# Opening handed on by tiles and halves, and POOL's follow-up steps placed a slot later, in a four-block transformer kernel

## Chip, core and metric

One core of a Trainium2 chip. The time is the device time of one execution in microseconds (us). Engines: PE (TensorE, matrix products), DVE (VectorE), ACT (ScalarE), POOL (GpSimd) and SP, which issues the transfers.

## What is computed

x has 4 batches of 512 tokens with 128 channels. Four residual layers follow each other; each first normalises x over its channels.

```python
x = x + attn_a(layernorm(x))   # channel attention, 8 heads of 16 channels: rms norm, q and k normalised over tokens
x = x + ffn(layernorm(x))      # 8 experts of 336 hidden, a router, a small actor net that says how many experts count
x = x + attn_b(layernorm(x))   # token attention, one head, scores times a step function of sigmoid
x = x + ffn(layernorm(x))      # the same expert weights again

# attn_a
q, k = l2norm(q), l2norm(k)    # over the tokens
sim  = einsum('bhin,bhjn->bhij', q * exp(temperature), k)
out  = einsum('bhij,bhjn->bhin', softmax(sim), v) @ w_out.T
# ffn
scores = where(rank < sampled_k, softmax(x @ router_w.T), 0)
for e in range(8):
    out += scores[..., e] * ((silu(x @ gate_w[e].T) * (x @ up_w[e].T)) @ down_w[e].T)
```

## The kernel before

The main loop is the expert layer. Its 8 x 336 hidden units are 21 chunks of 128, and it runs over 8 blocks: block n is batch n of the first expert layer for n below 4, batch n - 4 of the second one behind. So there are 168 slots, k = 21 n + c. In a slot PE makes the gate product and the up product of chunk c (`gu k`), each as three float32r products of high and low halves (`three`, L1007 to L1009, 128 x 512 elements), and a down product of an earlier chunk in float32 (`down k`, L1157, two records for one product). ACT makes silu of the gate product into `sl` (L691), DVE multiplies the up product into `t2` (`uk k`, L953), POOL makes the second multiplication of `t2` in place (`um k`, L574), and the down product reads that. In blocks 0 to 2 (`ROUTED_LATE`) DVE multiplies by silu and POOL by the routing weights `sbc`; from block 3 on DVE multiplies by `sbc` and POOL by silu. The gate product of slot k needs silu k - 2, since two banks of PSUM alternate, and the up product needs `uk k - 2`.

Everything else is cut into steps that a planner, `plan` (L163), puts between the slots. The lists `A_STEPS`, `B_STEPS`, `F_STEPS` give for each step a slot from the start of its thread; `COST` and `POOL_COST` are rough costs by which a step is put off or a product `um` is let in. Each engine then walks the one common list of steps and issues its own share of each step, so the place of a step in the list is its place in every engine's queue. An engine that waits for a semaphore in one step holds up all that it has behind. The steps that matter here:

- `stats` (DVE mean and variance, L786 and L789), with POOL's reciprocal root in the same step (L519 to L524: from the fourth normalisation on four instructions, a multiplication, an affine, a power and a product). `xn` normalises: on DVE for the first three (L800), on ACT for the others (L594). `xT` transposes it on PE (L1027), ACT copies it as the high half (L614), `xl` makes the low half on DVE (L819).
- `ag`, `ar`, `asim` (PE L1040, L1048, L1055 and L1057): Gram product of xn, its product with the weights of q and k, the similarity with the sums of squares of q and k beside it. `ass` (DVE L842) takes the sums, POOL's power (L533) stands in the same step. `ascale` (DVE L849 qn and L850 simT) scales, `asT` transposes simT on PE (L1063), `amax`, `aexp`, `awo` (L872 the output weights), `am` (PE L1069), `am2`, `y` (PE L1085) and the addition to x (DVE L878) follow.
- `route` (PE L1097 and L1098): the router's products. They need the low halves of x and of the router's weights (`swl`, DVE L809 and L810). `actk` (DVE L937) ends in the choice of experts; POOL spreads it to the weights `sx` (L543) in the same step, and `sbc` transposes them.
- `warm`: products of the identity on PE (L1019), 12, 2, 4, 7 and 10 of them, whose results are not read.

`PRELUDE` (L75) is the opening, written out by hand: attention of batch 0, statistics of batch 1, and the normalisation of block 0 up to its low half. PE's other small products take turns in three banks of PSUM (4 to 6); `turn(t)` waits until the one three turns back is free. At its start POOL sets up the identity and constants; the head mask `hmask` of 24 small instructions (L491 to L494) comes after the first reciprocal root.

## Time and profile before

| | |
|---|---|
| median of 3 runs | 499.86 us (499.83 to 501.45) |
| the profiled execution | 500.62 us, span of its profile 498.8 us |
| PE busy | 484.0 us, 97% of the span |
| DVE, ACT, POOL busy | 294.1, 243.4, 292.1 us |

A row of the timeline has the start in us from the span's start, the length in us, the engine, the line, the operation, the tile written and the tiles read, the shape, and how many instructions are merged in it; in brackets the engine's idle time just before and what ended it. A float32 product of PE makes two records. PEld is PE's weight load. In a table of windows the stretch comes first, then its length, the busy time and count of each engine, and behind them PE's granted clock (1.00 is 2.4 GHz, 0.50 is 1.2 GHz).

### The profile page before, as it was taken

The page shows a single profiled execution, that of the slowest core. Times are in us where ns is not written, and L with a number is a line of the kernel's source. Part 1 is how long each engine was busy: PE and PEld are TensorE (multiplying, and loading weights), DVE is VectorE, ACT ScalarE, POOL GpSimd, SP SyncE. Part 2 cuts the span into 40 slices and gives each one's busy share as a digit, 9 for nine tenths or more (in the row PEclk, how much of TensorE's full clock was granted, in tenths as well). Part 3 has the DMA queues.
Part 4 walks back from the last instruction along what each step waited for, and adds up shares of the span by engine and source line. Part 5 has one row for each costly group of instructions (what it writes and reads, how often), then busy time and mean ns, then how long its engine had stood idle before and what let it go on. Part 6 is the DMA issues. An engine that isn't in the chain of part 4 may idle for free.

```text
span 498.8 us, 6344 instructions
## 1 busy us (share of the span) xinstructions
PE 484.0 (97%) x2035; PEld 340.1 (68%) x2035; DVE 294.1 (59%) x695; ACT 243.4 (49%) x437; POOL 292.1 (59%) x307
## 2 busy tenths in 40 slices
PE   7798899999999899999999999999999999999997
PEld 7676767677666666676676676667676676666666
DVE  3538343746768795497937985469763334623232
ACT  3185837457624874248742756326671344232221
POOL 4346779338868485464563656365563646655653
PEclk9899999999999999999999999999999999999999
DMA  8700000000000000000000000000000000000000
GB/s 240 237 0 2 0 1 1 0 1 1 1 1 1 1 0 1 0 1 1 0 1 1 0 2 0 1 0 24 0 1 0 1 23 0 0 1 21 1 1 21
DMA packets 7932, 7.36 MB, mean 15 GB/s; under 512 B 732, under 2 KB 7772, under 8 KB 7900
## 3 DMA queue, kind: packets, MB, share of 16 engines
q1 hardware_dynamic: 7900, 6.97, 4.6%
q8 instruction: 16, 0.26, 0.2%
q14 instruction: 16, 0.13, 0.1%
HBM read 5.91 MB, written 1.05 MB: 14 GB/s over the span
## 4 chain that ended last, share of the span: by engine, by line
PE 81%; DVE 2%; ACT 1%; issue 1%; POOL 0%; ACTq 0%; DVEq 0%
PE bank L1157 26%; PE bank L1007 15%; PE bank L1009 14%; PE bank L1008 14%; PE bank L1195 3%; PE bank L1187 1%; PE bank L1111 1%; PE bank L1027 1%; PE bank L1165 1%; PE bank L1207 1%; PE bank L1119 1%; PE bank L1145 1%; PE bank L1098 1%; PE bank L1097 0%; PE bank L1085 0%
## 5 line engine op out<-in xcount | busy, mean ns | idle before, releaser
L574 POOL TENSOR_TENSOR t<-t,sl 128x512 f32<-128x512 f32 x105 | 136.0, 1299 | 109.8 <-DVE t L953 93.4
L691 ACT ACTIVATE sl<-bank 128x512 f32<-128x512 f32 x168 | 99.3, 597 | 150.0 <-PE bank L1009 143.5
L1157 PE MATMUL bank<-t,WD 128*128 128x512 f32 x328 | 162.7, 591 | 0.0
L953 DVE TENSOR_TENSOR t<-bank,sbc 128x512 f32<-128x512 f32 x105 | 72.4, 690 | 93.7 <-PE bank L1009 92.5
L1007 PE MATMUL bank<-xhF,WGh 128*128 128x512 f32 x168 | 103.8, 618 | 3.0 <-ACT sl L691 2.2
L574 POOL TENSOR_TENSOR t<-t,sbc 128x512 f32<-128x512 f32 x63 | 81.9, 1326 | 11.2 <-ACT sbc L685 7.9
L1157 PEld LDWEIGHTS bank<-t,WD 128*128 128x128 f32 x328 | 61.8, 188 | 25.1 <-issue 13.0
L953 DVE TENSOR_TENSOR t<-bank,sl 128x512 f32<-128x512 f32 x63 | 42.8, 685 | 54.7 <-ACT sl L691 24.3
L1007 PE MATMUL bank<-xhF,WUh 128*128 128x512 f32 x168 | 66.5, 396 | 1.3 <-DVE t L953 1.3
L1009 PE MATMUL bank<-xhF,WGl 128*128 128x512 f32 x168 | 66.3, 395 | 0.0
L1009 PE MATMUL bank<-xhF,WUl 128*128 128x512 f32 x168 | 66.0, 393 | 0.0
L1008 PE MATMUL bank<-xlF,WGh 128*128 128x512 f32 x168 | 65.9, 392 | 0.0
L1008 PE MATMUL bank<-xlF,WUh 128*128 128x512 f32 x168 | 65.6, 390 | 0.0
L1007 PEld LDWEIGHTS bank<-xhF,WGh 128*128 128x128 f32 x168 | 31.8, 189 | 26.2 <-issue 21.1
L1008 PEld LDWEIGHTS bank<-xlF,WGh 128*128 128x128 f32 x168 | 31.8, 190 | 21.5 <-issue 19.9
L1007 PEld LDWEIGHTS bank<-xhF,WUh 128*128 128x128 f32 x168 | 31.5, 188 | 10.4 <-DVE t L953 3.5
L1009 PEld LDWEIGHTS bank<-xhF,WGl 128*128 128x128 f32 x168 | 31.5, 187 | 7.5
L1008 PEld LDWEIGHTS bank<-xlF,WUh 128*128 128x128 f32 x168 | 31.6, 188 | 7.2
L1009 PEld LDWEIGHTS bank<-xhF,WUl 128*128 128x128 f32 x168 | 31.5, 188 | 7.2
L691 ACT ACT_TABLE_LOAD x19 | 24.4, 1283 | 0.3
L519 POOL TENSOR_SCALAR nm<-mv 128x4 f32<-128x4 f32 x13 | 3.0, 230 | 26.6 <-DVE mv L789 26.5
L521 POOL TENSOR_TENSOR rstd<-rt,nhalf 128x4 f32<-128x4 f32 x16 | 16.6, 1035 | 1.3
(191 smaller groups left out, 636.8 us busy)
## 6 DMA issues: line engine op xcount, KB each, us to landing
stage<-in_gate SPq DMA_DIRECT2D x7, 192.0 KB, 6.1
stage<-in_up SPq DMA_DIRECT2D x7, 192.0 KB, 6.3
WD<-in_down SPq DMA_DIRECT2D x7, 192.0 KB, 6.2
X<-in_x SPq DMA_DIRECT2D x4, 256.0 KB, 5.5
out<-X SPq DMA_DIRECT2D x3, 256.0 KB, 2.3
raw<-in_small SPq DMA_DIRECT2D x1, 388.0 KB, 4.6
out<-X SPq DMA_DIRECT2D x2, 128.0 KB, 1.9
raw<-in_small SPq DMA_DIRECT2D x1, 192.0 KB, 2.7
```

The costliest lines, as they stand in the source:

```text
L521: r = pool.tensor_tensor(rstd[:, :], rt[:, :], nhalf[:, :], ALU.pow)
L574: pool.tensor_tensor(t2[k % NT2][:, :], t2[k % NT2][:, :], by[:, :], ALU.mult).then_inc(a_done, 1)
L691: act.activation(sl[k % NSL][:, :], bank[k % 2][:, :], ACT.Silu).then_inc(silu_done, 1)
L953: dve.tensor_tensor(t2[k % NT2][:, :], bank[2 + k % 2][:, :], by[:, :], ALU.mult).then_inc(t2_done, 1)
L1007: pe.matmul(out, lh, rh, start=start, stop=False)
L1008: pe.matmul(out, lh, rl, start=False, stop=False)
L1009: return pe.matmul(out, ll, rh, start=False, stop=stop)
L1027: r = pe.transpose(m[:, i * P:i * P + P], xn[:, i, :], ident[:, :])
L1098: r = pe.matmul(m[:, o + 2 * E:o + 3 * E], xl[:, a], router[:, 0:E], start=True, stop=True)
L1111: r = pe.matmul(m[:, 8 * i:8 * i + KMAX], hq[:, i * P:i * P + P], w2[:, 0:KMAX], start=True, stop=True)
L1157: pe.matmul(OACC[:, :], WD[:, c, :], t2[k % NT2][:, :], start=(c == 0), stop=(c == CH - 1 or k == TAIL[0] - 1))\
L1195: r = pe.matmul(m[:, :], xnB[b % 2][:, j, :], PT[:, j, :], start=(j == 0), stop=(j == NT - 1))
```

## The change

POOL's share of three steps becomes a step of its own: `rstd` (the reciprocal root), `apow` (the power of the norms) and `sx` (the spread of the experts' weights). In the lists they stand a slot behind the step that they were part of, before the step that reads them; `ascale` of batches 2 and 3 moves a slot too. In the opening the results are passed on in parts: xn of the first three normalisations by tiles; the sums of squares of batch 0 ahead of the similarity and in a bank of their own; y of batch 0 in four banks, added and measured by tiles; the transposed x of block 0 in two halves, with the first gate product's order changed so that both parts which need only the high half come first. Half of the head mask is made before the first reciprocal root.

```diff
-A_STEPS = [(0, "stats"), (2, "xn"), ... (8, "ass"), (9, "ascale"),
+A_STEPS = [(0, "stats"), (1, "rstd"), (2, "xn"), ... (8, "ass"), (9, "apow"), (10, "ascale"),
...
-POOL_COST = dict(wp=1.2, wc=1.5, um=1.4, stats=1.4, ass=.8, bqkl=1.4, actk=1.1, inner=1)
+POOL_COST = dict(wp=1.2, wc=1.5, um=1.4, rstd=1.4, apow=.8, bqkl=1.4, sx=1.1, inner=1)
...
             pool.memset(nhalf[:, :], -0.5).then_inc(consts_ready, 1)
+            head_mask(range(H // 2))
...
-                if kind == "stats":
+                if kind == "rstd":
...
                     if seq == 0:
-                        head_mask()
-                if kind == "ass":
+                        head_mask(range(H // 2, H)).then_inc(consts_ready, 1)
+                if kind == "apow":
...
-                if kind == "actk":
+                if kind == "sx":
...
+                    if (what, b) == ("F", 0):
+                        act.wait_ge(half_full, 1)
+                        act.activation(xhF[0][:, 0:T // 2], bank[3][:, 0:T // 2], ACT.Copy).then_inc(xh_half, 1)
...
                     for i in range(NT):
-                        r = dve.tensor_scalar(xn[:, i, :], X[:, NT * q + i, :], mv[:, i, 0:1], rstd[:, i:i + 1],
-                                              ALU.subtract, ALU.mult)
-                    r.then_inc(xn_ready, 1)
+                        dve.tensor_scalar(xn[:, i, :], X[:, NT * q + i, :], mv[:, i, 0:1], rstd[:, i:i + 1],
+                                          ALU.subtract, ALU.mult).then_inc(xn_ready, 1)
...
+                    if s == ("y", 0):
+                        for i in range(NT):
...
+                            r = dve.tensor_tensor(X[:, i, :], bank[i][:, 0:P], X[:, i, :], ALU.add)
...
+                    to = m if b else bank[1]
                     for j in range(2):
-                        r = pe.matmul(m[:, P + j:P + j + 1], qsq[:, 1 - j, :], ones[:, :], start=True, stop=True)
+                        r = pe.matmul(to[:, P + j:P + j + 1], qsq[:, 1 - j, :], ones[:, :], start=True, stop=True)
+                    if b == 0:
+                        r.then_inc(squares_full, 1)
+                        r = pe.matmul(m[:, 0:P], raw[:, C_QKV + P:C_QKV + 2 * P], gw[:, 0, :], start=True, stop=True)
...
+                    if k == 0:
+                        pe.wait_ge(xh_ready, split_no["F", 0] + 1)
+                        pe.matmul(bank[0][:, :], WGh[:, 0, :], xhF[0][:, :], start=True, stop=False)
+                        pe.matmul(bank[0][:, :], WGl[:, 0, :], xhF[0][:, :], start=False, stop=False)
```

What this does to the engines' queues behind the opening shows in three places. DVE, slots 16 to 18, the scaling of batch 2 (qn, simT) among the multiplications `uk` into the sixteen buffers t2 (t20 is that of slot 16, t21 of slot 17); before:

```order
89 L842 TENSOR_SCALAR ss_139<-bank5 128x2
90 L953 TENSOR_TENSOR t20_114<-bank2,sl0_112 128x512
91 L786 BN_STATS bst_83<-X_49 128x6 x4
92 L789 BN_AGGR mv0_84<-bst_83 128x2 x4
93 L849 TENSOR_TENSOR qn_144<-rs_140,etemp_69 128x1
94 L850 TENSOR_SCALAR simT_141<-bank5,rs_140 128x128
95 L953 TENSOR_TENSOR t21_115<-bank3,sl1_113 128x512
96 L953 TENSOR_TENSOR t22_116<-bank2,sl0_112 128x512
```

and now:

```order
93 L867 TENSOR_SCALAR ss_139<-bank5 128x2
94 L990 TENSOR_TENSOR t20_114<-bank2,sl0_112 128x512
95 L802 BN_STATS bst_83<-X_49 128x6 x4
96 L805 BN_AGGR mv0_84<-bst_83 128x2 x4
97 L990 TENSOR_TENSOR t21_115<-bank3,sl1_113 128x512
98 L875 TENSOR_TENSOR qn_144<-rs_140,etemp_69 128x1
99 L876 TENSOR_SCALAR simT_141<-bank5,rs_140 128x128
100 L990 TENSOR_TENSOR t22_116<-bank2,sl0_112 128x512
```

The scaling now stands behind the multiplication of slot 17. The same happens to batch 3 in slots 34 to 36. PE's queue still has the transposition of simT (`asT`) at its old place, behind the transposes of block 1.

PE, slots 48 to 49, the transposes of block 3 (ident, xn), which stood right behind the products of slot 49; before:

```order
436 L1009 MATMUL bank<-xhF_75,WGl 128x512
437 L1007 MATMUL bank<-xhF_75,WUh 128x512
438 L1008 MATMUL bank<-xlF_77,WUh 128x512
439 L1009 MATMUL bank<-xhF_75,WUl 128x512
440 L1027 MATMUL bank<-ident,xn_79 128x128 x4
441 L1007 MATMUL bank<-xhS,zh 128x512
```

and now:

```order
436 L1046 MATMUL bank<-xhF_75,WGl 128x512
437 L1044 MATMUL bank<-xhF_75,WUh 128x512
438 L1045 MATMUL bank<-xlF_77,WUh 128x512
439 L1046 MATMUL bank<-xhF_75,WUl 128x512
440 L1217 MATMUL bank<-t_121,WD 128x512
441 L1067 MATMUL bank<-ident,xn_79 128x128 x4
442 L1044 MATMUL bank<-xhS,zh 128x512
```

Down product 39 has gone ahead of the transposes; it had stood a slot later. In the same way down product 23 is now ahead of the transposes of batch 0 for the second attention (slot 36) and of `asT` behind them.

POOL, slots 62 to 64, the reciprocal root of block 4 (nm, rt, rstd, nmr) among the products `um` (t215 is that of slot 63, t20 of slot 64); before:

```order
166 L574 TENSOR_TENSOR t214_128<-t214_128,sbc0_110 128x512
167 L519 TENSOR_SCALAR nm0_90<-mv0_84 128x4
168 L520 TENSOR_SCALAR rt0_88<-mv0_84 128x4
169 L521 TENSOR_TENSOR rstd0_86<-rt0_88,nhalf_72 128x4
170 L524 TENSOR_TENSOR nmr0_92<-nm0_90,rstd0_86 128x4
171 L574 TENSOR_TENSOR t215_129<-t215_129,sl1_113 128x512
172 L574 TENSOR_TENSOR t20_114<-t20_114,sl0_112 128x512
```

and now:

```order
166 L578 TENSOR_TENSOR t214_128<-t214_128,sbc0_110 128x512
167 L578 TENSOR_TENSOR t215_129<-t215_129,sl1_113 128x512
168 L578 TENSOR_TENSOR t20_114<-t20_114,sl0_112 128x512
169 L523 TENSOR_SCALAR nm0_90<-mv0_84 128x4
170 L524 TENSOR_SCALAR rt0_88<-mv0_84 128x4
171 L525 TENSOR_TENSOR rstd0_86<-rt0_88,nhalf_72 128x4
172 L528 TENSOR_TENSOR nmr0_92<-nm0_90,rstd0_86 128x4
```

Two products now stand ahead of the root, and each of them waits for DVE's multiplication of its slot. ACT's queue has the same steps in the same places in both kernels; only the copy of block 0's high half is now two.

## Rows read from the trace of the kernel before

**Rows 1.** The page, busy time by engine, share of the span, instructions.

```profile
PE 484.0 (97%) x2035; PEld 340.1 (68%) x2035; DVE 294.1 (59%) x695; ACT 243.4 (49%) x437; POOL 292.1 (59%) x307
```

**Rows 2.** PE's waits from 27 us: total us, times, longest us.

```profile
PE bank L1007 <- ACT sl L691: 2.2, 2, 1.7
```

**Rows 3.** Windows of the opening; PE's granted clock is behind POOL.

```profile
15.00:16.00 1.00, 1.00 (x6) 1.00 (x6) 0.50 (x3) 0.43 (x2) 0.00 (x0) 0.50 1.09 354
```

**Rows 4.** Timeline, attention of batch 0 in the opening.

```profile
6.37 1.11 DVE L800 TENSOR_SCALAR xn<-X,mv,rstd 128x128 f32<-128x128 f32 x4 [1.52 <-POOL rstd L521]
...
7.54 1.16 PE L1040 MATMUL bank<-xn 128*128 128x128 f32 x8 [0.52 <-DVE xn L800]
...
10.92 0.46 PE L1055 MATMUL bank<-gw,raw 128*128 128x128 f32 x2 [0.65 <-DVE qsq L833]
...
11.22 0.50 PE L1057 MATMUL bank<-ones,qsq 128*128 128x1 f32 x4
...
11.76 0.16 DVE L842 TENSOR_SCALAR ss<-bank 128x2 f32<-128x2 f32 x1 [0.98 <-PE bank L1057]
...
12.11 0.34 POOL L494 TENSOR_SCALAR_AFFINE_SELECT hmask<-hmask 128x16 f32<-128x16 f32 x1
12.41 0.70 POOL L533 TENSOR_TENSOR rs<-ss,nhalf 128x2 f32<-128x2 f32 x1
...
13.89 3.19 PE L1019 MATMUL bank<-ident 128*128 128x128 f32 x14
...
15.66 0.28 DVE L872 TENSOR_SCALAR wo<-raw,ari 128x128 f32<-128x128 f32 x1
...
16.88 0.43 PE L1069 MATMUL bank<-wo,attn 128*128 128x128 f32 x2
```

**Rows 5.** Timeline, from y of batch 0 to the first routing product.

```profile
18.55 1.16 PE L1085 MATMUL bank<-mixw,xaT 128*128 128x128 f32 x8 [0.37 <-ACT mixw L653]
...
19.74 0.69 DVE L878 TENSOR_TENSOR X<-bank,X 128x512 f32<-128x512 f32 x1 [2.16 <-PE bank L1085]
...
24.41 1.10 PE L1027 MATMUL bank<-ident,xn 128*128 128x128 f32 x8 [0.44 <-DVE xn L800]
...
25.11 0.60 ACT L614 ACTIVATE xhF<-bank 128x512 fp32r<-128x512 f32 x1 [0.35 <-PE bank L1027]
...
26.99 0.28 DVE L810 TENSOR_TENSOR SWl<-raw,SWh 128x128 fp32r<-128x128 f32 x1
...
28.04 0.17 PE L1097 MATMUL bank<-router,xhF 128*128 128x16 f32 x1
```

**Rows 6.** Timeline, slots 17 to 19: normalisation of block 1, transposition of batch 2's similarity.

```profile
70.10 1.65 ACT L594 ACTIVATE xn<-X,nmr,rstd 128x128 f32<-128x128 f32 x4 [4.05 <-POOL nmr L524]
...
72.30 0.27 PE L1063 MATMUL bank<-ident,simT 128*128 128x128 f32 x1
...
72.32 1.29 DVE L953 TENSOR_TENSOR t<-bank,sl 128x512 f32<-128x512 f32 x2 [3.99 <-issue]
```

**Rows 7.** Timeline, slots 34 to 37: scaling of batch 3, next gate product.

```profile
119.57 1.27 POOL L574 TENSOR_TENSOR t<-t,sbc 128x512 f32<-128x512 f32 x1
...
119.63 1.22 DVE L849 TENSOR_TENSOR qn<-rs,etemp 128x1 f32<-128x1 f32 x1 [0.50 <-POOL rs L533]
...
123.49 0.50 PE L1007 MATMUL bank<-xhF,WGh 128*128 128x512 f32 x1 [0.51 <-ACT sl L691]
```

**Rows 8.** Timeline, slots 49 to 51: high half, down products, routing product of block 3.

```profile
161.20 0.60 ACT L614 ACTIVATE xhF<-bank 128x512 fp32r<-128x512 f32 x1 [0.54 <-PE bank L1027]
...
163.08 1.88 PE L1157 MATMUL bank<-t,WD 128*128 128x512 f32 x4
...
167.97 0.28 PE L1097 MATMUL bank<-router,xhF 128*128 128x16 f32 x1 [0.76 <-DVE xlF L819]
```

**Rows 9.** Timeline, slots 65 to 68: normalisation of block 4, silu behind it, a gate product.

```profile
217.64 1.64 ACT L594 ACTIVATE xn<-X,nmr,rstd 128x128 f32<-128x128 f32 x4
...
219.18 0.58 ACT L691 ACTIVATE sl<-bank 128x512 f32<-128x512 f32 x1
...
222.97 0.48 PE L1007 MATMUL bank<-xhF,WGh 128*128 128x512 f32 x1
```

More of the change, by code:

```diff
@@ L398, in build @@
         xn_act = sem("xn_act")
+        half_full, xh_half = sem("half_full"), sem("xh_half")
+        squares_full = sem("squares_full")
+        y0_tile, x0_tile = sem("y0_tile"), sem("x0_tile")
         m_full = [sem(f"m_full{i}") for i in range(3)]
@@ L427, in wait_free, with wait_xn @@
             eng.wait_ge(m_free[t % 3], t // 3 + 1)
-        def wait_xn(eng, seq):
+        def wait_xn(eng, seq, tile=NT - 1):
             if seq < DVE_NORMS:
-                eng.wait_ge(xn_ready, seq + 1)
+                eng.wait_ge(xn_ready, NT * seq + tile + 1)
             else:
@@ L485, in chain, with head_mask @@
                 pool.wait_ge(pool_did, did[0])
-            def head_mask():
-                for e in range(H):
+            def head_mask(heads):
+                for e in heads:
                     own = hmask[:, e * DH:e * DH + DH]
@@ L613, in _ @@
                     dst = xhF[b % 2] if what == "F" else xhS
+                    if (what, b) == ("F", 0):
+                        a = slice(T // 2, T)
+                        act.activation(dst[:, a], m_bank(t)[:, a], ACT.Copy).then_inc(xh_ready, 1)
+                        continue
                     act.activation(dst[:, :], m_bank(t)[:, :], ACT.Copy).then_inc(xh_ready, 1)
@@ L777, in _ @@
                         dve.wait_ge(x_loaded[q], 16)
-                    else:
+                    elif (what, b) != ("F", 0):
                         wait_free(dve, turn_of[src])
@@ L785, in _ @@
                     for i in range(NT):
+                        if (what, b) == ("F", 0):
+                            if i < NT - 1:
+                                dve.wait_ge(x0_tile, i + 1)
+                            else:
+                                wait_free(dve, turn_of[src])
                         r = dve.bn_stats(bst[:, i, :], X[:, NT * q + i, :])
@@ L815, in _ @@
                     dst, hi = (xlF[b % 2], xhF[b % 2]) if what == "F" else (xlS, xhS)
+                    if (what, b) == ("F", 0):
+                        a = slice(0, T // 2)
+                        dve.wait_ge(xh_half, 1)
+                        dve.tensor_tensor(dst[:, a], bank[3][:, a], hi[:, a].bitcast(F32), ALU.subtract)
+                        a = slice(T // 2, T)
+                        dve.wait_ge(xh_ready, split_no["F", 0] + 1)
+                        dve.tensor_tensor(dst[:, a], m_bank(t)[:, a], hi[:, a].bitcast(F32), ALU.subtract).then_inc(n_free(t), 1)
+                        continue
                     dve.wait_ge(xh_ready, split_no[what, b] + 1)
@@ L1022, in _ @@
                     t = turn_of[s]
-                    wait_xn(pe, norm_no[what, b])
-                    xn = xnB[b % 2] if what == "B" else xns[norm_no[what, b] % 2]
+                    seq = norm_no[what, b]
+                    xn = xnB[b % 2] if what == "B" else xns[seq % 2]
                     m = turn(t)
                     for i in range(NT):
-                        r = pe.transpose(m[:, i * P:i * P + P], xn[:, i, :], ident[:, :])
+                        if i == 0 or seq < DVE_NORMS:
+                            wait_xn(pe, seq, i if seq < DVE_NORMS else NT - 1)
+                        to = bank[3] if (what, b) == ("F", 0) and i < NT // 2 else m
+                        r = pe.transpose(to[:, i * P:i * P + P], xn[:, i, :], ident[:, :])
+                        if (what, b, i) == ("F", 0, NT // 2 - 1):
+                            r.then_inc(half_full, 1)
                     r.then_inc(m_full[t % 3], 1)
@@ L1084, in _ @@
                         a = slice(i * P, i * P + P)
-                        r = pe.matmul(m[:, a], xaT[b % 2][:, a], mixw[:, :], start=True, stop=True)
+                        to = m[:, a] if b else bank[i][:, 0:P]
+                        r = pe.matmul(to, xaT[b % 2][:, a], mixw[:, :], start=True, stop=True)
+                        if b == 0 and i < NT - 1:
+                            r.then_inc(y0_tile, 1)
                     r.then_inc(m_full[t % 3], 1)
@@ L1130, in _ @@
                         pe.wait_ge(silu_done, k - 1)
-                    three(bank[k % 2][:, :], WGh[:, c, :], WGl[:, c, :], xh, xl).then_inc(g_full, 1)
+                    if k == 0:
+                        r = pe.matmul(bank[0][:, :], WGh[:, 0, :], xl, start=False, stop=True)
+                    else:
+                        r = three(bank[k % 2][:, :], WGh[:, c, :], WGl[:, c, :], xh, xl)
+                    r.then_inc(g_full, 1)
                     if k >= 2:
```

56 lines of the change are left out of this document (35 added, 21 removed).

## Prediction, made before the changed kernel was run

> **What bounds the kernel now.** I read the page's busy shares first: TensorE (PE) is busy 484.0 of 498.8 us, no other engine over 60% [rows 1]. So past the opening only what makes PE wait can change the time. The waits of PE after 27 us come next; the largest is for ScalarE's silu, twice, 2.2 us in all [rows 2]. Third, the timeline of the opening: there PE works through a chain of small steps in which one engine hands to the next, and fills the gaps with warm-up products of the identity that nobody reads. Steps that end earlier there move the whole main loop. Fourth, the timeline at the places where the planner's order is different. The granted clock of PE in the opening is the last view: from 15 to 16 us it is 0.50, the 1.2 GHz level [rows 3].
>
> **The opening, part by part.** (a) *xn passed on by tiles.* DVE writes four tiles of xn in 1.11 us from 6.37, and the Gram product starts only at 7.54, eight records in 1.16 us [rows 4]. With 0.27 for the last record that is 0.11 per record. Now it ends two records after the fourth tile, not eight: 6 x 0.11 = 0.67 us earlier. The warm-up ahead of it is nearly done when the first tile comes, so the last tile decides. (b) *Squares first.* The two column sums start 0.30 after the 128-wide product in front of them (10.92 and 11.22). They now stand ahead of it: 0.30. (c) *Half of the head mask before the statistics.* The norms' sums end at 11.92, but POOL's power starts at 12.41, behind the last select of the mask (12.11 for 0.34) [rows 4]. The handover from DVE to PE at 7.48 and 7.54 costs under 0.1, so 0.4 comes free. Half of the mask moves into POOL's wait for the first statistics, so the other half is done well ahead of the power. (d) *The warm-up in front of the attention's product.* The weights of the output product are ready at 15.94 (15.66 plus 0.28), the product starts at 16.88: fourteen warm-up records took 3.19 us, 0.21 each, at half clock [rows 3, 4]. With the chain 1.4 earlier they start at 12.5 and end between 14.1 (all at the higher level) and 14.5 (the fall again near 13.5), before the weights at 14.6. Another 0.86 goes. (e) *y in tiles.* One addition of 0.69 follows the eight records of y [rows 5]. In four parts, the last one overhangs by a quarter plus its fixed cost, some 0.2 to 0.3: 0.5 with the handover. (f) *Halves of the transposed x.* ScalarE copies it from 25.11 for 0.60, DVE makes the low part, then PE starts the first gate product. In halves that path is up to 1.3 shorter. But the routing product at 28.04 also needs the low router weights, which DVE finishes at 27.27 behind the squares of batch 1 [rows 5]; those wait for ScalarE's other copies, which start only 0.3 earlier. So PE gains 28.04 - 27.27 - 0.1 + 0.3 = 0.95, and I take that.
>
> Sum: 0.67 + 0.30 + 0.40 + 0.86 + 0.50 + 0.95 = 3.7 us. The upper bound is 4.0 (1.3 for the last term). Below: the second long warm-up, ten products in twenty records, stands in front of batch 1's Gram product and the transposes. If the low clock falls on it, each record costs 0.1 more, 2 us; over half of that has cover, since PE still waited for xn behind it, 0.44 us before the transposes at 24.41 [rows 5] and more before the Gram product. I count 0.8. Before the fall of 13.5 PE had worked in short pieces; the new chain has its thin stretch, the same three small products, just ahead of that warm-up. I take 3.4 us, between 3.7 and 2.9.
>
> **The steps moved to a later slot.** Most of it costs nothing: for the expansion of the weights POOL had been idle, so products now go first. Three places are not free.
>
> *First place, the second scaling (batch 2), slots 16 to 18.* DVE now has product 17's multiplication ahead of qn and simT. That multiplication waits for silu 17, and silu 17 stands on ScalarE behind a normalisation (70.10 for 1.65). It ran at 72.32 [rows 6]. PE takes simT at 72.30, right after the transposes. Before, simT was ready long ahead. Now it comes at 72.32 + 0.61 (the next issue) + 0.4 = 73.35, so PE waits 1.1 us, and nothing behind it has slack, as PE is never idle there. Ends: 1.1, and 2.2 if qn is held up.
>
> *Second place, the third scaling, slots 34 to 36.* The same: the multiplication ahead of it waits for a silu, and PE itself waited 0.51 for that silu at 123.49 [rows 7]. simT comes near 124.6, PE goes on at 124.75. A down product (0.86) now stands ahead and fills PE's gap, so the loss is 124.75 - 123.49 - 0.86 = 0.4. Ends: 0.4 and 1.2.
>
> What both upper ends rest on: qn, a product of one column, took 1.22 us at 119.63 and ended with POOL's product of 119.57 [rows 7]. In the new places POOL has its products back to back. The Trainium skill, GPSIMD Engine Reference, section Key points, says that GpSimd shares its SBUF interfaces with VectorE and contends with DVE instructions that have two SBUF inputs; the row agrees, with 1.22 us. By that rule the two losses would be nearer 1.4 and 1.1. I take 1.2 and 0.7, between the free case and the row.
>
> *Third place, the transposes of block 3, slot 49.* The down product 39 is now ahead of them. Four records of down take 1.88, the last one 0.59, so 0.43 a record and 0.86 for one product. ScalarE's copy at 161.20 had waited for these transposes; behind it in its queue stand a table load, two exponentials, a second table load and silu, and the routing product at 167.97 waited 0.76 for what follows [rows 8]. All of that moves by 0.86, PE's other work does not grow: 0.85 us lost. Ends: 0 (if another wait is last) and 0.9.
>
> Sum of the body: 1.2 + 0.7 + 0.85 = 2.75 us, ends 1.5 and 4.3. Fewer waits on POOL are a gain only where PE waits for POOL, and no such wait is in the list of PE's waits, of which the largest is shown [rows 2].
>
> The profiled execution's own time is 500.62 us (span 498.8), 0.76 above the median of the three runs. The sum is a difference: 500.62 - 3.4 + 2.75 = 499.97, less 0.76 against the median: 499.2. I predict 499.2 us, with 497.2 to 501.3 as this case's own range (4.0 - 1.5 = 2.5 in favour; 2.9 - 4.3 = 1.4 against).
>
> **Rivals.** *The body stays as it is.* The late scalings are hidden, because silu 17 comes earlier than I think or a later wait swallows the loss; only the opening counts: 499.86 - 3.4 = 496.5. For it: a shifted PE often meets its next wait later. Against: PE is 97% busy [rows 1], there is hardly a wait to swallow anything.
>
> *The clock.* The lower level stays over all twenty records of the long warm-up and over the transposes: the opening gives 3.7 - 2.2 = 1.5, the total is 499.86 - 1.5 + 2.75 = 501.1. For it: the opening before had such a stretch too [rows 3]; against: PE is busier between 10 and 13.5 us than before.
>
> *The slower side.* In the blocks whose products need both multiplications in another order (from block 3 on), POOL's product waits for DVE's of the same slot. The reciprocal roots now stand behind it. At 217.64 ScalarE normalises for 1.64 us [rows 9]; its inputs would now be ready at 219.6, 2 us later, and every silu behind shifts by 2. The silu at 219.18 lasts 0.58; the gate product that needs it starts at 222.97, so 3.2 us of slack remain [rows 9] and the shift is covered with 1.2 left. This decides it: if more than 1.2 us of other delay meets it, PE waits. Four blocks have this pattern; at 1 us each the total is 503.3.
>
> *That the change doesn't do what it says* is small: the instructions' order shows the moves in the places named.
>
> **How the numbers follow.** Forecast 0.68, body unharmed 0.12, clock 0.12, slack used up 0.08. The range 497.2 to 501.9 takes in the forecast with its ends and the clock case, and leaves out 0.12 below and 0.08 above. Half a per cent, 2.5 us, is about what a measurement of this kernel can tell from no change: under 497.4 lies the unharmed body and a sliver of the forecast, 0.13; over 502.4 the used slack, 0.09; between them 0.78.
>
> **What would show it.** The routing product, at 28.04 before, should start near 24.6 (24.3 to 25.1). POOL's first power of the norms near 11.0 instead of 12.41. Then, counted from that routing product: PE waits over 1 us for simT in the third transposition of the similarity, 0.5 to 1.2 in the fourth, and the wait for the low half of x in block 3 grows from 0.76 to 1.6. In blocks 4, 5, 7 the normalisation on ScalarE starts up to 2 us later, with no wait of PE behind it. Wrong would be: a routing product later than 26, or PE waits over 1 us after 200 us.

## The result and the profile after

The changed kernel takes 502.56 us, the median of six runs (501.88 to 503.29); before, run beside it, took 499.85. The ratio is 1.0042, with a 95% interval from 1.0028 to 1.0055: slower by 0.42%. The forecast was 499.2, its range ended at 501.9. The profiled execution is the fastest of the six, 501.88 us with a span of 500.1, and PE's mean granted clock is 1.00 in it; four of the other five have 0.997. Run again later (experiment 15) it took 502.61; the medians of before beside the experiments lie between 499.92 and 500.63.

The opening after, rows of the timeline that answer [rows 4] and [rows 5]. Columns are as there:

```profile
6.69 1.26 PE L1084 MATMUL bank<-xn 128*128 128x128 f32 x8 [0.45 <-DVE xn L816]
...
10.17 0.58 PE L1103 MATMUL bank<-ones,qsq 128*128 128x1 f32 x4 [0.65 <-DVE qsq L856]
...
10.79 0.16 DVE L867 TENSOR_SCALAR ss<-bank 128x2 f32<-128x2 f32 x1 [0.76 <-PE bank L1103]
...
11.03 0.94 POOL L537 TENSOR_TENSOR rs<-ss,nhalf 128x2 f32<-128x2 f32 x1 [1.75 <-DVE ss L867]
...
12.65 1.73 PE L1056 MATMUL bank<-ident 128*128 128x128 f32 x14
...
14.37 0.29 DVE L898 TENSOR_SCALAR wo<-raw,ari 128x128 f32<-128x128 f32 x1
...
14.76 0.46 PE L1118 MATMUL bank<-wo,attn 128*128 128x128 f32 x2 [0.39 <-issue]
```

```profile
16.98 0.96 DVE L908 TENSOR_TENSOR X<-bank,X 128x128 f32<-128x128 f32 x4 [0.69 <-PE bank L1135]
...
21.11 1.44 PE L1067 MATMUL bank<-ident,xn 128*128 128x128 f32 x8 [0.37 <-DVE xn L816]
...
21.64 0.38 ACT L609 ACTIVATE xhF<-bank 128x256 fp32r<-128x256 f32 x1
...
23.99 0.28 DVE L825 TENSOR_TENSOR SWl<-raw,SWh 128x128 fp32r<-128x128 f32 x1
24.33 0.28 PE L1149 MATMUL bank<-router,xhF 128*128 128x16 f32 x1
```

The routing product starts at 24.33, not 28.04: 3.71 us earlier. And yet the kernel is slower. So I set every up product of PE beside its counterpart in the trace before (start after less start before, in us):

| up product of slot | difference | step | what lies between |
|---|---|---|---|
| 2 to 18 | -3.61 | | the opening |
| 19 to 36 | -2.30 | +1.3 | second scaling (slot 30 apart, where a down product is counted early) |
| 45 to 49 | -0.07 | +2.2 | third scaling and what follows |
| 52 to 58 | +0.77 | +0.85 | down product 39 ahead of the transposes |
| 59 to 110 | +1.10 | +0.3 | the second attention's turn at 192.4 |
| 111 to 165 | +1.26 to +1.30 | +0.2 | normalisation of block 6 |

The body lost 4.9 us (3.61 and 1.26). PE's waits from 25 us on name the places (total us, times, longest); the third answers [rows 2], where it was 2.2 us, twice:

```profile
PE bank L1067 <- DVE simT L876: 1.9, 1, 1.9
PE bank L1149 <- DVE xlF L842: 1.6, 1, 1.6
PE bank L1044 <- ACT sl L702: 1.6, 1, 1.6
PE bank L1044 <- DVE t L990: 1.3, 1, 1.3
PE bank L1112 <- DVE simT L876: 1.0, 1, 1.0
PE bank L1118 <- issue: 0.7, 1, 0.7
PE bank L1225 <- DVE bmp L1017: 0.7, 1, 0.7
```

The first place, the timeline that answers [rows 6]. The multiplication of product 17 is ahead of qn and simT, and PE's transposition of simT waits for all three:

```profile
68.72 0.69 DVE L990 TENSOR_TENSOR t<-bank,sl 128x512 f32<-128x512 f32 x1 [4.30 <-issue]
...
69.32 0.22 DVE L875 TENSOR_TENSOR qn<-rs,etemp 128x1 f32<-128x1 f32 x1
...
69.47 0.34 DVE L876 TENSOR_SCALAR simT<-bank,rs 128x128 f32<-128x128 f32 x1
...
69.96 0.30 PE L1112 MATMUL bank<-ident,simT 128*128 128x128 f32 x1 [1.04 <-DVE simT L876]
```

The second place, answering [rows 7]. Here the one that waits is not the transposition of simT (L1112, at 123.33) but the four transposes of block B0 ahead of it (L1067), which don't read simT. And on DVE pr, a product of 128x32, takes 2.70 us:

```profile
121.23 0.69 DVE L990 TENSOR_TENSOR t<-bank,sl 128x512 f32<-128x512 f32 x1 [4.39 <-ACT sl L702]
121.84 0.69 DVE L875 TENSOR_TENSOR qn<-rs,etemp 128x1 f32<-128x1 f32 x1
122.45 0.34 DVE L876 TENSOR_SCALAR simT<-bank,rs 128x128 f32<-128x128 f32 x1
...
122.84 0.66 PE L1067 MATMUL bank<-ident,xnB 128*128 128x128 f32 x4 [1.85 <-DVE simT L876]
...
123.33 0.27 PE L1112 MATMUL bank<-ident,simT 128*128 128x128 f32 x1
...
123.69 5.02 POOL L578 TENSOR_TENSOR t<-t,sbc 128x512 f32<-128x512 f32 x4
...
126.06 2.70 DVE L939 TENSOR_TENSOR pr<-pe__96,p 128x32 f32<-128x32 f32 x1
```

The third place, answering [rows 8]: the copy is 0.77 later than before, the routing product 0.78, and its wait has grown from 0.76 to 1.62:

```profile
161.97 0.60 ACT L625 ACTIVATE xhF<-bank 128x512 fp32r<-128x512 f32 x1 [1.39 <-PE bank L1067]
...
168.75 0.28 PE L1149 MATMUL bank<-router,xhF 128*128 128x16 f32 x1 [1.62 <-DVE xlF L842]
```

### The profile page after: what moved, and what is told of

Same layout as the page of the kernel before. It is cut to its first block, busy times and chain, and to the rows that moved or that the text cites. A ratio compares the mean times of both kernels' runs of the same rounds, so it can differ in the third digit from the quotient of the medians.

```text
span 500.1 us, 6349 instructions
## 1 busy us (share of the span) xinstructions
PE 482.6 (97%) x2035; PEld 337.8 (68%) x2035; DVE 294.9 (59%) x699; ACT 243.2 (49%) x438; POOL 291.8 (58%) x307
## 4 chain that ended last, share of the span: by engine, by line
PE 71%; DVE 3%; issue 1%; DVEq 0%
PE bank L1217 23%; PE bank L1044 13%; PE bank L1046 13%; PE bank L1045 13%; PE bank L1255 3%; PE bank L1247 1%; PE bank L1163 1%; PE bank L1067 1%; PE bank L1267 1%; PE bank L1225 1%; PE bank L1205 1%; PE bank L1171 1%; DVE t L990 0%; DVE ge L948 0%; PE bank L1150 0%
## 5 line engine op out<-in xcount | busy, mean ns | idle before, releaser
L598 ACT ACTIVATE xn<-X,nmr,rstd 128x128 f32<-128x128 f32 x36 | 14.8, 483 | 10.0 <-POOL nmr L528 10.0
L1003 DVE TENSOR_SCALAR mk<-bank 128x512 bf16<-128x512 f32 x16 | 11.0, 689 | 11.1 <-PE bank L1046 10.9
```

The lines of the kernel that those rows point to most:

```text
L598: r = act.activation(xn[:, i, 0:n], X[:, NT * (b % NB) + i, 0:n], ACT.Identity, bias=nmrs[seq % 2][:, i:i + 1], scale=rstds[seq % 2][:, i: ...
L1003: dve.tensor_scalar(jumps[:, :], x_, X25 / 10, 2.0, ALU.is_ge, ALU.mult).then_inc(mk_ready, 1)
```

## Experiments

Fifteen of them, in four series (1 to 4, 5 to 8, 9 to 12, 13 to 15), each with its own executions of before, to which the ratios refer. The changed kernel's own row is from its first six executions. "Full clock" counts the executions whose mean granted clock is 0.999 or 1.000; "us at full clock" is their middle.

| experiment | median us | ratio to before, 95% | full clock | us at full clock |
|---|---|---|---|---|
| the changed kernel | 502.56 | 1.0042 (1.0028 to 1.0055) | 2 of 6 | 501.9 |
| 1 opening only | 497.39 | 0.9941 (0.9924 to 0.9958) | 5 of 6 | 497.4 |
| 2 moved steps only | 506.74 | 1.0120 (1.0099 to 1.0140) | 0 of 5 | - |
| 3 scalings back | 501.55 | 1.0026 (1.0013 to 1.0039) | 0 of 12 | - |
| 4 asT a product later | 502.76 | 1.0045 (1.0029 to 1.0061) | 2 of 7 | 502.2 |
| 5 = 3, pr by four | 505.12 | 1.0081 (1.0054 to 1.0107) | 0 of 6 | - |
| 6 = 3, POOL's order back | 503.30 | 1.0035 (1.0005 to 1.0065) | 2 of 12 | 498.6 |
| 7 down 39 back | 501.23 | 1.0007 (0.9989 to 1.0025) | 10 of 12 | 501.2 |
| 8 three places mended | 503.11 | 1.0053 (1.0032 to 1.0074) | 1 of 9 | 502.1 |
| 9 = 3, POOL waits | 498.26 | 0.9945 (0.9928 to 0.9963) | 5 of 12 | 497.7 |
| 10 = 1, POOL waits | 497.26 | 0.9936 (0.9915 to 0.9957) | 7 of 8 | 497.2 |
| 11 = 3 + 7, POOL waits | 497.36 | 0.9943 (0.9921 to 0.9965) | 4 of 7 | 497.1 |
| 12 before, POOL waits | 500.31 | 1.0000 (0.9985 to 1.0016) | 6 of 12 | 499.8 |
| 13 changed, POOL waits | 501.55 | 1.0024 (1.0003 to 1.0045) | 5 of 12 | 501.0 |
| 14 = 10 + down 23 | 496.35 | 0.9912 (0.9876 to 0.9947) | 6 of 6 | 496.4 |
| 15 changed, again | 502.61 | 1.0041 (1.0021 to 1.0061) | 4 of 12 | 502.1 |

### The two halves of the change, experiments 1 and 2

Experiment 1 puts the new steps back into their old slots (and "sx" in the three lists of F in the same way):

```diff
-A_STEPS = [(0, "stats"), (1, "rstd"), ... (8, "ass"), (9, "apow"), (10, "ascale"),
+A_STEPS = [(0, "stats"), (0, "rstd"), ... (8, "ass"), (8, "apow"), (9, "ascale"),
-B_STEPS = [(0, "stats"), (1, "rstd"), ...
+B_STEPS = [(0, "stats"), (0, "rstd"), ...
-           (15, "actk"), (16, "sx"), (18, "sbc")]
+           (15, "actk"), (15, "sx"), (18, "sbc")]
```

> The changed opening with every engine's body in the order of before (the new POOL steps stand in the slot of the step that they were cut from). Theory: the opening alone gives what the two profiles show, and its size depends on the clock. Against the profiled run of before, whose warm-up ran at half clock, it was 3.7 us; 0.76 of that lay only in this profiled run (500.62 against a median of 499.86), so against the median it should be 2.95 us: 496.9 us, between 496.7 and 497.1. Silu should stand 3.6 us earlier than in the profile of before from slot 8 to the end. Rival 1, the half clock is in every run of before: the whole 3.7 us, 496.2. Rival 2, the shifted PE meets its later waits and gives part back in the body: 497.5 to 499.0, with the lead over before shrinking along the slots.

Measured 497.39, with the up products 3.2 us ahead of before's from slot 2 to slot 165, without a loss on the way. The rival that the shifted PE gives part back is out. The time lies 0.3 above my interval, and in part for a reason that the trace shows: in its trace PE's first 24 warm-up records took 5.49 us (4.53 in the changed kernel's), so the Gram product started at 6.99, not at 6.69.

Experiment 2 is the kernel before with the changed step lists and POOL costs, nothing of the opening.

> The opening of before, with the moved steps. Theory: the moved steps cost 5.0 us in the body whatever the opening (2 times 1.3 and 2.2 for the scalings, 0.85 for the down product, 0.5 for later roots; the sum of the silu differences is 3.61 + 1.28 = 4.9): 499.85 + 4.9 = 504.8 us, 504.4 to 505.2. Rival: part of the loss comes from the new opening (a slot that starts earlier meets a load or a copy that did not), then under 504.0.

Measured 506.74, a miss: 1.5 above the interval, and none of its executions kept the full clock. Only its fastest one, 505.28 at a mean clock of 0.997, has a trace; the median lies 1.5 above that, at 0.993, and what the others lost beyond it isn't in any trace. In the trace the steps between slots are those of the changed kernel, +1.3, +2.2, +0.85, +0.3 and +0.2, and 0.7 for a stretch at the low clock level behind slot 51. So the moved steps cost the same 4.9 us with the old opening. It also shows the opening of before at full clock. The warm-up in front of the attention's product and the routing product:

```profile
13.84 1.73 PE L1019 MATMUL bank<-ident 128*128 128x128 f32 x14
...
27.14 0.17 PE L1097 MATMUL bank<-router,xhF 128*128 128x16 f32 x1
```

The fourteen records take 1.73 us, not the 3.19 of [rows 4], and the routing product starts at 27.14, 0.90 earlier than in the profiled execution of before. So the low level of [rows 3] is not in every execution of before's opening. The profiled execution of experiment 12, whose opening is before's too, had it at the same place, from 13.8 us on, and took 500.80; at full clock both kernels take 499.8.

### The late scalings, experiments 3 and 4

Experiment 3 swaps two pairs in the planner's list, which moves nothing but DVE's instructions:

```diff
+    steps.remove(('uk', 17))
+    steps.insert(steps.index(('ascale', 2)) + 1, ('uk', 17))
+    steps.remove(('uk', 35))
+    steps.insert(steps.index(('ascale', 3)) + 1, ('uk', 35))
     return steps, order
```

> The changed kernel with two instructions pairs swapped on DVE only: the scaling of batch 2 stands ahead of multiplication 17, that of batch 3 ahead of multiplication 35, as before. Theory: both waits of PE for simT go (1.04 at 69.96 and 1.85 at 122.84), 1.3 + 2.2 = 3.5 us at most, of which 0.5 may come back as the wait for silu that stood at 123.49 before: 502.56 - 3.0 = 499.6, between 499.0 and 500.1. Rival: the second place is not DVE's order but the down product that moved ahead of the transposes there, so ScalarE's copy stays late: only the 1.3 of the first place comes back, 501.2.

Measured 501.55: a miss for the theory, near the rival's 501.2, though not for the rival's reason. Slot 19 had its 1.3 back. Slot 37 had its own 2.1 back as well: up product 37 stood 3.36 ahead of before, 0.15 in the changed kernel. But between slots 39 and 45 three microseconds went again. DVE and POOL there, and the wait of PE that came of it:

```profile
122.88 4.74 DVE L943 TENSOR_TENSOR pr<-pe__96,p 128x32 f32<-128x32 f32 x1
```

```profile
122.59 4.97 POOL L582 TENSOR_TENSOR t<-t,sbc 128x512 f32<-128x512 f32 x4
```

```profile
PE bank L1048 <- DVE xlS L846: 1.9, 1, 1.9
```

pr took 4.74 us, where its shortest of eight is 0.19, and ended with the fourth of four POOL products in a row. Behind it on DVE stand gt, ge and the low half xlS, and PE's products of the second attention that come next read xlS. My texts for experiments 5 and 9 call this a wait for silu; the row says xlS.

Experiment 4 asks who waited in the second place of the changed kernel. On PE, asT of batch 3 goes behind the gate and up products of slot 37, and the transposes stay:

```diff
+    steps.remove(('asT', 3))
+    steps.insert(steps.index(('gu', 37)) + 1, ('asT', 3))
     return steps, order
```

> The changed kernel with the fourth transposition of the similarity (asT 3) one gate and up product later on PE, and all else as it is. Theory: in the second place what PE waits for is not the similarity but the bank that the transposes of block B0 take, which the scaling still holds; so PE waits at the transposes as before the edit (1.9 us, near 122.8) and the time stays within 0.3 of 502.56. Rival, which is how the prediction told it: PE waits for simT at asT 3; then the wait moves behind 2.3 us of products and is gone, 500.7 to 501.3.

```profile
PE bank L1069 <- DVE simT L878: 1.8, 1, 1.8
```

The wait is still there, still at the transposes, and the time is 502.76. The theory holds. `turn` lets a step have one of three banks only when the step three turns back has freed it, and what lies three turns ahead of the transposes of B0 is the similarity of batch 3, freed by the late scaling. ScalarE's copy of B0, behind the transposes, is late with them.

### The held DVE instructions, experiments 5, 6, 8, 9, 10, 12 and 13

Experiment 5 is experiment 3 with

```diff
-                    chain(dve.tensor_tensor(pr[:, :, :], pe_[:, :, :], p4[:, 2].unsqueeze(2).to_broadcast([P, NT, E]), ALU.mult))
+                    for i in range(NT):
+                        r = dve.tensor_scalar(pr[:, i, :], pe_[:, i, :], p4[:, 2, i:i + 1], None, ALU.mult)
+                    chain(r)
```

> Experiment 3 (both scalings back in front), with the probabilities pr formed by four products with one value per partition instead of one product of two tiles. Theory: in the trace of experiment 3 pr took 4.74 us instead of 0.19, ended with the fourth POOL product in a row, and PE then waited 2.5 us for silu at 126.5; four products that read one tile each don't meet this, so the wait shrinks to the 0.5 to 0.8 that before had there, and the time falls by 1.7 to 2.0: 499.5 to 499.9 where experiment 3 had 501.5. Rival 1, the products with a value per partition are held as well: no change. Rival 2, gt and ge behind it, which read pr twice, are held in its stead: 0.5 or less.

505.12: worse. The four products took 4.73 us together, again to the end of POOL's row, and in other blocks they added waits (0.5 at slot 8, 0.8 more at slot 59). Rival 1: products of a tile by a value per partition are held too. But they were held differently: each of the four ended with one POOL product (the last three took 1.33, 1.31 and 1.25), where the single pr of experiment 3 lasted through four. Four instructions can be held four times, and in block 3 all four were, each lasting 1.3 us. Experiment 8 had the same edit beside the other two mended places, and missed for the same reason (5.13 us for pr, PE paused 2.9):

> The changed kernel with three places mended: both scalings back in front, down product 39 back, pr by four products with one value per partition. Everything else of the moved steps is kept. Theory: of the 4.9 us that the moved steps cost, these three places hold 1.3 + 2.2 + 0.85; what is left is 0.5, from roots that stand behind products (slots 58 and 111): 497.4 + 0.5 = 497.9, 497.5 to 498.3. Rival: the moved steps cost in many small places, then over 498.8.

Experiment 6 is experiment 3 with three POOL steps moved back, so that POOL's order around slots 32 to 35 is before's:

```diff
+    steps.remove(('rstd', 'B', 0))
+    steps.insert(steps.index(('um', 22)) + 1, ('rstd', 'B', 0))
+    steps.remove(('apow', 3))
+    steps.insert(steps.index(('um', 23)) + 1, ('apow', 3))
+    steps.remove(('inner', 2, 0))
+    steps.insert(steps.index(('um', 24)) + 1, ('inner', 2, 0))
```

> Experiment 3 with the order of three POOL steps as before around slots 32 to 35: the reciprocal root of block B0 and the power of batch 3 in front of products 23 and 24, the inner step of block 2 behind product 24. PE keeps the down product 23 in its new place. Theory: pr falls between POOL's products again (0.4 us as in experiment 1), the wait of 2.5 us goes down to 0.8 or less, 499.5 to 499.9. Rival, the down product in front of the transposes makes ScalarE's copy and the silu behind it late by 0.86: PE still waits 1.5 us or more there, 500.4 or more.

Its twelve executions fall in two groups: four from 498.5 to 500.1, eight from 503.0 to 505.2. The profiled one is of the upper group. pr kept its 0.39, as in experiment 1; the next one, a comparison, did not:

```profile
123.39 6.36 DVE L953 TENSOR_TENSOR gt<-pr 128x256 bf16<-128x256 f32 x1
```

It takes 0.42 when nothing holds it. Here it ended at 129.75, 0.3 behind the last of five POOL products back to back (one of the actor net and four `um`), and PE paused 4.1 us. So the same program seems to hold gt in one execution and not in another, and 3 us hang on it (500.1 and 503.0 at the same mean clock of 0.997). Only an execution of the upper group has a trace. In that of experiment 1, gt began as closely behind the actor net's product (0.13 us, here 0.15), and four `um` followed that one there too; yet it took 1.49.

Experiment 9 takes away the cause. In experiment 3, POOL may not begin the row before DVE is through:

```diff
                     n = k // CH
+                    if k == 29:
+                        pool.wait_ge(pr_ready, 3)
                     pool.wait_ge(t2_done, k + 1)
```

> Experiment 3 (both scalings back in front, POOL's new order kept) with one more wait: POOL's product 29 waits until DVE has made pr and both comparisons of block 2. Theory: in experiments 3, 5 and 6 a DVE instruction of this group (pr for 4.7 us, gt for 6.4) lasted until a row of back-to-back POOL products ended, and PE then waited 2.5 to 4.1 us for silu. If the row cannot start before them, pr takes 0.2 and gt 0.4, the wait goes down to 0.8 or less, and the time is 2.2 us under experiment 3: 498.6 where the clock stays up, 499.3 with one stretch at the low level. Rival, the long DVE instruction is waiting for something else (the exponentials' exchange, a semaphore) that the trace merges into it: the same 501.5. Second rival, the delay of POOL's products costs PE as much: 500.5 or more.

```profile
122.99 0.19 DVE L945 TENSOR_TENSOR pr<-pe__96,p 128x32 f32<-128x32 f32 x1
123.21 0.42 DVE L949 TENSOR_TENSOR gt<-pr 128x256 bf16<-128x256 f32 x1
...
124.05 5.01 POOL L584 TENSOR_TENSOR t<-t,sbc 128x512 f32<-128x512 f32 x4 [1.30 <-DVE ge L950]
```

pr and gt are back to 0.19 and 0.42, POOL begins its row 1.5 us later, and the kernel takes 498.26 where experiment 3 took 501.55. The gain is 3.3 us in the medians, 2.9 between the traces, more than the 2.2 expected, since the late DVE had also delayed the attention product of batch 3 (PE's 0.7 at L1118). Both rivals are out: the long instruction waited for POOL's row, and POOL's delay costs PE nothing that the trace shows.

> The changed kernel with nothing but POOL's product 29 behind the comparisons of block 2. Theory: the second place lost 2.2 us in the changed kernel, and only 1.2 of it is the wait for the bank that the late scaling holds; the other 1.0 comes from pr, held for 2.7 us by a row of POOL products (PE waits 0.45 for silu at 129.7, and the attention product of batch 3 comes 0.7 late at 136.4). With POOL waiting, 1.0 us is won: 500.9 at full clock where the changed kernel has 501.9. Rival: all of the 2.2 is the bank's wait and what it pushes; the time stays at 501.9 at full clock.

Experiment 13 is the changed kernel with that wait alone. At full clock it takes 501.0 against 501.9: 0.9 us won, and the wait of 1.9 for the bank stays. That divides the second place: 1.2 us for the bank, 1.0 for the held pr.

> Experiment 1 (changed opening, body as before) with the same wait of POOL's product 29. Theory: in the trace of experiment 1 gt and ge took 1.49 and 1.51 us and PE's waits near there were not for them, so the median stays at 497.3 (497.0 to 497.6), and no execution lies 2 us or more above it. Rival, POOL's products come 1 us later and PE waits for a down product: 498 or more.

497.26, as expected: the wait costs nothing where nothing is held.

> The kernel before with POOL's product 29 behind the comparisons of block 2. Some executions of before at full clock lie 2.2 us above the others (499.7 and 501.9 on the last chip). Theory: this is the same hold of a comparison by a row of POOL products, which meets some executions only; with the wait no execution at full clock lies above 500.5, median 499.8. Rival: the second level is made elsewhere, and stays.

None of its twelve lies above 501.4, where of the 26 of before beside it two at full clock had 502.0 and two more 503.6. That fits the theory; but with 4 in 26 (16 in 93 over all four series), none in 12 can be chance, so it isn't settled that before's upper group is this hold. No execution of that group has a trace.

### Down products and the clock, experiments 7, 15, 11 and 14

Experiment 7 is the changed kernel with down product 39 behind gate and up product 50 again:

```diff
+    steps.remove(('down', 39))
+    steps.insert(steps.index(('gu', 50)) + 1, ('down', 39))
     return steps, order
```

> The changed kernel with down product 39 behind the transposes of block 3 again, one slot later. Theory: PE's pause ahead of the routing product of block 3 goes from 2.2 us (166.5) back to 1.35, 0.85 us less in each execution, so 501.0 to 501.2 where PE's clock stays up; and because PE's low level followed just behind that pause in the traces of experiments 2 and 3 (169.0 and 173.4), fewer executions show a clock under 1.0, which takes the median down further, 501.1 against 502.5. Rival 1, another wait is last there: 502.3 or more. Rival 2, the low level has nothing to do with the pause: the share of such executions stays at half or more, median 501.6.

At full clock 501.2, 0.7 to 0.9 less than the changed kernel, and ten of twelve executions kept the full clock. Rival 1 is out. A pause is counted here, and in the texts, from the start of PE's last record to the next one; the idle time in a row's brackets is 0.3 to 0.6 less.

> The changed kernel as it is, for its share of executions at full clock beside that of experiment 7, which took PE's 2.2 us pause ahead of the routing product of block 3 down to 1.35. Theory: with the pause, half or fewer of the executions keep the full clock (501.9), the others lie at 502.6; experiment 7 kept it in 10 of 12. Rival: the pause has no part in it; the share is that of experiment 7 or higher, and the median is 501.9.

Four of twelve at full clock (502.1), the others mostly at 502.6. Its profiled execution is one of these. PE's granted clock (third number from the end) by windows:

```profile
167.00:168.00 1.00, 0.33 (x1) 0.00 (x0) 0.39 (x1) 1.00 (x3) 0.00 (x0) 1.00 0.00 0
168.00:169.00 1.00, 0.05 (x1) 0.05 (x1) 1.00 (x3) 0.50 (x2) 0.00 (x0) 1.00 0.00 0
...
170.00:171.00 1.00, 1.00 (x6) 0.82 (x6) 0.97 (x3) 0.16 (x1) 0.00 (x0) 0.95 0.00 0
171.00:172.00 1.00, 1.00 (x4) 0.81 (x3) 0.93 (x4) 1.00 (x3) 0.00 (x0) 0.50 0.00 0
```

PE does little for two windows, resumes at 168.95, and near 170.9 the clock goes to 0.50, the 1.2 GHz level, until about 174.3. Products come 0.43 apart instead of 0.23 there. The traces of experiments 2, 3, 6, 9 and 13 show the same behind the same pause, those of 5, 6 and 8 behind the pause of 2.5 to 4.1 us that the held DVE made; in that of experiment 4 the low level began at 50.1, at the end of a pause of 1.9 us that every one of the kernels has. Of the kernels with the 2.2 us pause at slot 51 (changed twice, 2, 3, 4, 9, 13) 18 of 66 executions kept the full clock; of those with 1.35 us there (1, 7, 10, 11, 14) 32 of 39, and with before and experiment 12, which have 1.35 us there too, 103 of 144. The series ran on different chips, but before kept the full clock in 20 of 26 beside experiment 7 and in 18 of 23 beside experiment 15, so it is hardly the chip that makes 10 of 12 and 4 of 12 of them; these two differ by one product moved. The length of the pause isn't all: the changed kernel, 2, 4, 7 and 13 have one of 2.4 to 2.5 us at the second place (120.4 to 122.84 in the changed kernel's trace), and in none of their traces does the low level follow it. What sets the pauses apart was not tried.

> The changed kernel with both scalings back in front, down product 39 back, and POOL's product 29 behind the comparisons of block 2; all else of the moved steps is kept. Theory: this mends the three places by their causes, and of the 4.9 us of the body 0.5 are left (roots behind products, slots 59 and 111), 497.8 (497.5 to 498.2), nearly all executions at full clock. Rival: the moved steps cost more in small places, 498.8 or more.

497.36, and 497.1 at full clock, a little better than the theory (though three of seven executions, not nearly none, fell below it): with the three places mended by their causes, the moved steps are as good as the old ones, and 0.5 is left in small places (0.33 at slot 59 and 0.17 at slot 111 in its trace too). That it isn't worse than experiment 10 is down product 23:

> Experiment 10 (changed opening, old places, POOL's wait) with one of the moved PE steps alone: down product 23 in front of the transposes of block B0. Theory, as the prediction credited it: the product (0.86 us) fills PE's wait for silu there (0.78 at 119.5), so 0.8 us less than experiment 10: 496.5 at full clock. Rival: ScalarE's copy behind the transposes comes later and silu 38 with it, the wait moves on by one slot: 497.1 or more.

Experiment 14 moves it alone (`('down', 23)` behind `('gu', 36)` in experiment 10). 496.35, all six executions between 496.29 and 496.74: 0.9 us less than experiment 10, the credit is real. PE's wait for silu there is gone: 2.1 us in two waits in the list of experiment 10, 1.6 in one here. This is the best version, 0.9912 of before.

## Why the prediction was wrong

A gain of 0.7 us was forecast and a loss of 2.7 came. The opening did what was said; the sum missed in the offset to the median, in the second place, and in small places and a stretch of low clock that stood at nothing.

**The opening, terms (a) to (f): right against the profiled execution.** ss starts at 10.79, 0.97 earlier (0.67 + 0.30 said); the power stands 0.24 behind it, not 0.65, at 11.03 (near 11.0 said), which is 0.41 (0.40 said). From the power to the attention's product it is 3.73, not 4.47: 0.74 (0.86 said; the power itself took 0.94, before 0.70). y's additions end 1.48 behind its first record, not 1.88: 0.40 (0.50 said). The rest, to the routing product at 24.33, is 1.2 (0.95 said). 3.71 us against a sum of 3.7. That the sum fits to 0.01 is luck: the misses of -0.12, -0.10 and +0.24 cancel. The 1.3 us by which the halves were to shorten the path to the gate product, the upper bound of (f), stands in no row. The low level, for which I took 3.4 instead of 3.7, did not fall on the long warm-up in this trace.

**How it stands to the median: wrong, 0.6 us.** The step that failed is "less 0.76 against the median". The profiled execution of before was slower than its median because of the low level in the fourteen warm-up records, and term (d), 0.86, removed just that. I took the same 0.8 to 0.9 us off twice: once as gain, once as offset. Experiment 2 shows before's opening without it, routing at 27.14. Against the median the opening is worth 27.14 - 24.33 = 2.8 us, not 3.4. Experiment 1 gave 2.4 in the measured times, full clock against full clock (3.2 between the medians, since 8 of the 18 executions of before beside it had a lower clock).

**First place: right in the mechanism.** 1.2 said, 1.3 found, PE waited 1.04 (1.1 said). But the 0.1 that I added for a held qn isn't what made it more than 1.1: qn took 0.22 and was not held.

**Second place: wrong, 1.5 us.** 0.4 to 1.2 said, 0.7 taken, 2.2 found. Two steps failed. I let PE go on until asT and put the down product of 0.86 into its gap; but the transposes ahead of asT needed the bank that the scaling held (experiment 4), so PE stood 1.85 us with the product already done. The credit itself was right, as experiment 14 shows; the loss beside it was larger, 1.2 net. And I looked for the hold by POOL on qn only, with the 1.22 of [rows 7] as its size. It fell on pr, two slots later; pr took 2.70, and that cost 1.0 (experiment 13).

**Third place: right.** 0.85 said, 0.85 found, the wait from 0.76 to 1.62 (0.76 to 1.6 said). What I had at nothing is the clock behind it. The median execution has a mean clock of 0.997, and takes 502.56 against 501.9: 0.65 us. The one such execution of the changed kernel with a trace (experiment 15) has it behind this pause, and without the longer pause ten of twelve kept the full clock (experiment 7); where the others have it isn't in a trace.

**Roots behind products.** In block 4 the row says what the rival worked out:

```profile
220.77 1.65 ACT L598 ACTIVATE xn<-X,nmr,rstd 128x128 f32<-128x128 f32 x4 [3.42 <-POOL nmr L528]
...
222.33 0.58 ACT L702 ACTIVATE sl<-bank 128x512 f32<-128x512 f32 x1
...
224.08 0.48 PE L1044 MATMUL bank<-xhF,WGh 128*128 128x512 f32 x1
```

217.64 plus the shift of 1.10 is 218.74; ScalarE starts at 220.77, 2.03 later, and 1.2 us are left between silu's end at 222.91 and the gate product. No wait of PE over 1 us follows after 200 us, and blocks 4, 5 and 7 moved nothing. In block 6, which I had not counted, the root behind a product moved the time by 0.17. And at slot 59 the turn of a bank came late:

```profile
192.45 0.63 PE L1247 MATMUL bank<-ident,Sb 128*128 128x128 f32 x4 [0.23 <-DVE xlS L842]
```

xlS was late on DVE behind a rank product (ge by tri) of 1.81 us among POOL's products, 0.33 in all. Whether each of these is the moved root or POOL's other order was not tried apart.

Together: 0.6 for the doubled offset, 1.5 for the second place, 0.6 for what I had at nothing or rounded (0.1 + 0.33 + 0.17), 0.65 for the clock: 3.35 of the 3.36 us between 499.2 and 502.56. The parts come from single traces and are good to 0.1 or 0.2 each, so the fit is closer than they are. The range was too narrow below its upper end for the same reasons: its body bound of 4.3 lay under the 4.9 found, and the doubled offset shifted all of it down. Its lower end has a slip besides: 2.5 us under 499.86 is 497.4, not 497.2.

## What to carry to other kernels

Ahead of taking the difference between a profiled execution and the median as an offset, find what made it: here it was the very stretch that the change shortened. When a step that frees a buffer moves, look at who takes that buffer next in turn, and not only at who reads the step's result. And where POOL has several products back to back, keep short DVE work that others wait for out of the row's way: one semaphore wait on POOL gave 3.3 us in experiment 9 and 0.9 in the changed kernel itself.

## What the runs showed of the hardware

**A row of POOL instructions can hold a DVE instruction to the row's end.** pr took 0.19 us alone, 2.70 among three POOL products and 4.74 among four; gt 0.42 alone, 1.49 in experiment 1 and 6.36 in experiment 6. In the trace of before no held instruction took over 2.2 us, and the qn of [rows 7] ended with a single POOL product; four products with a value per partition were held for one each, 4.73 us together. DVE's multiplications that read a PSUM bank kept 0.69 beside the same POOL products, at 121.23 in the changed kernel for one. The Trainium skill, SBUF — State Buffer, section SBUF: two separate sides, says that VectorE instructions with two SBUF inputs and GpSimd instructions that read SBUF take a shared pair of ports as an exclusive lock, and that whichever starts first has it for its whole instruction. The traces agree on the blocking, but for pr and gt in the row at issue the hold did not end with the POOL instruction it began in: in experiments 3 and 6 it went through four and five of them. Why gt was held through one in experiment 1 and through five in experiment 6, with starts alike within 0.02 us, was not explained.

**PE's low clock level came behind pauses of 1.9 to 4.1 us in a stretch in which PE is otherwise busy throughout,** in some executions and not in others, and not behind each such pause (experiment 7 has one of 2.4 us and kept the full clock). What such a stretch costs depends on the waits behind it. In experiment 15 eight products come 0.2 us later each, but the wait of 0.7 for bmp, which stands in the changed kernel's list of waits above, is gone with it, and 0.7 us remain. In experiment 4, with no such wait behind it, it cost 1.5 us (slots 12 and 13).
